# First stage of a three-stage attention kernel: per-tile x loads, mask product last, weight split one slot later, another order of the first loads

## The chip, the cores and the metric

The kernel runs on one core of a Trainium2 chip. The metric is the device time of one execution in microseconds (us); lower is better. Engines are named as the profile names them: PE (TensorE), DVE (VectorE), ACT (ScalarE), POOL (GpSimd) and SP (SyncE, which here only issues DMAs).

## What is computed

The input x holds 32 batches of 64 tokens by 512 features, and each batch has its own 256 context rows of 512 features and a mask. Three blocks follow one another, each added to its input:

```
x = x + cross_attention(layernorm(x), ctx, mask)   # scores over 256 context rows, softmax, read-out
x = x + latent_attention(layernorm(x), weights)    # low-rank q and kv, rotary part, 16 heads, causal
x = x + ffn(layernorm(x), weights)                 # square of relu, an expert sum, a layernorm
```

Everything is float32. Products that must be exact are made as three products of a rounded part and a remainder ("hi" and "lo").

## The kernel before

Three stages run one after another: `phase_x`, `phase_m` and `phase_f`. Only `phase_x` is touched. It does the cross-attention, the second layernorm and the low-rank projection z. Its unit is a pair of batches, that is 128 tokens, so there are 16 pairs. All 16 tiles of x (256 KB each) have a place of their own in `x_all`; the context rows (`ctx_in`, 1 MB a pair) and their transpose (`ctxT`, 1 MB a pair) have two places each, used in turn.

Every engine runs its own list of instructions, slot by slot, and semaphores tie the lists together. `slots` calls slot 0 to 18: slots 0 to 2 and 13 to 18 are written out, and those between run in a loop. The pairs are staggered. In slot p:

- PE: scores of pair p, read-out of p-1, transpose of the normalised x of p+1, projection of p-2, transpose of the probabilities of p, transpose of the second norm of p-1 (`turn1`, which waits for ACT's `norm`). Only then come the scores of p+1.
- DVE: remainder of the probabilities of p-1 (`probs_lo`), remainder of the second transpose (`turned1_lo`), layernorm statistics of x of pair p+2 (`first_var`), `latent_var`, `maximum` of the scores of p, `residual` and second statistics of p-1, then smaller work.
- POOL: half of the remainder of the context of p (`ctx_split`), 1/sqrt of the variance for p+2 (`rstd_of(0, p+2)`, from `first_var`), `latent_rstd`, the other half of `ctx_split`, `rstd_of(1, p-1)` (from the second statistics), `rotate(p-3)`.
- ACT: `probs_hi`, `turned1_hi`, first norm of p+1, squares, `exp`, `scale_q`, copy of the transposed x, `ctx_round` of p+1 (1.9 us), second norm of p-1.
- SP: in this order, load of `ctxT` for p+2 (after the scores of p), store of z of p-3 (after `rotate(p-3)`), store of the x of p-1 (after `residual`), load of `ctx_in` for p+2 (after all of `ctx_split(p)`).

Before slot 0, SP issues the first loads, in the order of the diff's minus and context lines; the last is x of pairs 4 to 15 in one DMA of 3 MB (line 172). The latent weights `w_raw` (1.1 MB) are rounded by ACT and their remainder is made by DVE at the end of slot 0 (lines 339 and 353). The scores begin with a small product that puts in the mask (line 500), which needs the loaded table `picks`.

Of the kernel before, what the change touches and what calls it, by code (L numbers as in the profile page):

```python
# [28 lines left out]
KH = HID // P  # L29
# [32 lines left out]
def phase_x(nc, A, scratch, early):  # L62

    with ExitStack() as ctx:
# [12 lines left out]
        def bank(name):  # L77
# [39 lines left out]
        b_z = [bank("z0"), bank("z1")]  # L117

        s = {n: ctx.enter_context(nc.semaphore("x_" + n)) for n in (
            "x_first x_second x_third x_rest masks_loaded small_loaded w_loaded ctxT_first0 ctxT_first1 ctxT_loaded0 ctxT_loaded1 "  # L120
            "ctx_loaded0 ctx_loaded1 x1_stored "
            "z_stored0 z_stored1 pool_setup consts masks_built w_hi w_lo "
            "stats0 var0 eps0 rstd0 shift0 norm0 turned0 xT0 stats1 var1 eps1 rstd1 shift1 norm1 turned1 xT1_hi xT1_lo "
# [13 lines left out]
        def has(p):  # L137

            return not isinstance(p, int) or 0 <= p < PAIRS
# [10 lines left out]

        @block.sync
        def _(sp):
            sp.dma_start(x_all[:, 0], x_t[0]).then_inc(s["x_first"], 16)
            for h in range(2):
                sp.dma_start(ctxT[:, 0, 2 * h:2 * h + 2], A["ctx_turned"][0, :, 2 * h:2 * h + 2]).then_inc(s[f"ctxT_first{h}"], 16)
            sp.dma_start(mask_u8[:], A["mask_BxS2_bk0"]).then_inc(s["masks_loaded"], 16)
            sp.wait_ge(s["pool_setup"], 2)
            sp.dma_start(picks[0:BATCH + 2].rearrange("p a n -> p (a n)"), A["picks"]).then_inc(s["masks_loaded"], 16)
            sp.dma_start(x_all[:, 1], x_t[1]).then_inc(s["x_second"], 16)
            sp.dma_start(ctx_in[:, 0], A["ctx_rows"][0]).then_inc(s["ctx_loaded0"], 16)  # L160
            sp.dma_start(ctxT[:, 1], A["ctx_turned"][1]).then_inc(s["ctxT_loaded1"], 16)
            sp.dma_start(x_all[:, 2:4], x_t[2:4].rearrange("t p d -> p t d")).then_inc(s["x_third"], 16)
            sp.dma_start(w_raw[:], A["w_latent"].rearrange("(k p) n -> p k n", p=P)).then_inc(s["w_loaded"], 16)
            sp.dma_start(ctx_in[:, 1], A["ctx_rows"][1]).then_inc(s["ctx_loaded1"], 16)
            for half in range(2):
                rows = slice(SEQ * half, SEQ * half + SEQ)
                sp.dma_start(cos[rows, :], A["rope_cos"]).then_inc(s["small_loaded"], 16)
                sp.dma_start(sin[rows, :], A["rope_sin"]).then_inc(s["small_loaded"], 16)
            sp.dma_start(qkv_b[:, 0:QLR], bcast_rows(A["L0_attn_wq_a_b"])).then_inc(s["small_loaded"], 16)
            sp.dma_start(qkv_b[:, QLR:ZW], bcast_rows(A["L0_attn_wkv_a_b"])).then_inc(s["small_loaded"], 16)  # L170
            sp.dma_start(kv_w[:], bcast_rows(A["L0_attn_kv_norm_w"])).then_inc(s["small_loaded"], 16)
            sp.dma_start(x_all[:, 4:], x_t[4:].rearrange("t p d -> p t d")).then_inc(s["x_rest"], 16)

            def load_ctxT(p, par):
                sp.wait_ge(s["scored"], p - 1)
                sp.dma_start(ctxT[:, par], A["ctx_turned"][p]).then_inc(s[f"ctxT_loaded{par}"], 16)

            def load_ctx(p, par):
                sp.wait_ge(s["ctx_lo"], 4 * (p - 1))
                sp.dma_start(ctx_in[:, par], A["ctx_rows"][p]).then_inc(s[f"ctx_loaded{par}"], 16)  # L180

            def store_z(p, par):
                sp.wait_ge(s["z_kv"], p + 1)
                sp.wait_ge(s["z_rope"], p + 1)
                sp.wait_ge(s["q_scaled"], p + 1)
                sp.dma_start(z_t[p], zbuf[:, par]).then_inc(s[f"z_stored{par}"], 16)

            def slot(p, par):
                if isinstance(p, int) and p == PAIRS - 1:
                    early.start(sp)  # L190
                if has(p + 2):
                    load_ctxT(p + 2, par)
                if has(p - 3):
                    store_z(p - 3, 1 - par)
                if has(p - 1):
                    sp.wait_ge(s["x1_done"], p)
                    sp.dma_start(x1_t[p - 1], x_all[:, p - 1]).then_inc(s["x1_stored"], 16)
                if has(p + 2):
                    load_ctx(p + 2, par)

            slots(sp, slot)
            for par in range(2):
                sp.wait_ge(s[f"z_stored{par}"], 8 * PAIRS)
            sp.wait_ge(s["x1_stored"], 16 * PAIRS)
# [66 lines left out]
        def _(act):  # L271
# [47 lines left out]
            def slot(p, par):  # L319
                if has(p - 1):  # L320
                    probs_hi(p - 1)
                if has(p - 2):
                    turned1_hi(p - 2)
                if has(p + 1):
                    norm(0, p + 1, xn0, x_all[:, p + 1])
                if has(p - 3):
                    squares(p - 3, 1 - par)
                if has(p):
                    exp(p)
                if has(p - 3):  # L330
                    scale_q(p - 3, 1 - par)
                if has(p + 1):
                    turned0(p + 1)
                    ctx_round(p + 1, 1 - par)
                if has(p - 1):
                    norm(1, p - 1, xn1, x_all[:, p - 1])
                if isinstance(p, int) and p == 0:
                    act.wait_ge(s["w_loaded"], 16)
                    a.copy(w_hi[:].rearrange(flat), w_raw[:].rearrange(flat)).then_inc(s["w_hi"], 1)

# [6 lines left out]
        def _(dve):  # L347
# [7 lines left out]
            def var(k, p, src):  # L355

                n = count(dve, held, p + 1)
                v.bn_stats(stats[k][:], src).then_inc(s[f"stats{k}"], 1)
                dve.wait_ge(s["x_first"], 16)
                dve.wait_ge(s[f"shift{k}"], p)  # L360
                dve.wait_ge(s[f"stats{k}"], n)
                v.bn_aggr(mean_var[k][:], stats[k][:]).then_inc(s[f"var{k}"], 1)
                dve.wait_ge(s[f"var{k}"], p + 1)
                if k == 0:
                    v.tensor_scalar(var_eps[k][:], mean_var[k][:, 1:2], float(HID), HID * 1e-5, ALU.mult, ALU.add).then_inc(s["eps0"], 1)
                else:
                    v.tensor_scalar(var_eps[k][:], mean_var[k][:, 1:2], 1e-5, None, ALU.add).then_inc(s["eps1"], 1)

            def first_var(p):
                if isinstance(p, int):  # L370
                    dve.wait_ge(s["x_first" if p < 1 else "x_second" if p < 2 else "x_third" if p < 4 else "x_rest"], 16)
                else:
                    dve.wait_ge(s["x_rest"], 16)
                var(0, p, x_all[:, p])

            def latent_var(p):
# [35 lines left out]
            def residual(p):  # L412
                dve.wait_ge(s["read"], p + 1)
                dve.wait_ge(s["validated"], p + 1)
                v.scalar_tensor_tensor(x_all[:, p], b_read[:], rvalid[:], x_all[:, p], ALU.mult, ALU.add).then_inc(s["x1_done"], 1)
                dve.wait_ge(s["x_first"], 16)
                dve.wait_ge(s["x1_done"], p + 1)
                var(1, p, x_all[:, p])

# [10 lines left out]
            def slot(p, par):  # L430
# [2 lines left out]
                if has(p - 2):  # L433
                    turned1_lo(p - 2)
                if has(p + 2):
                    first_var(p + 2)
                if has(p - 3):
                    latent_var(p - 3)
                if has(p):
# [6 lines left out]
                    latent_kv(p - 3, 1 - par)  # L446
                if has(p - 2):
                    bias(p - 2, par)
                if isinstance(p, int) and p == 0:
                    dve.wait_ge(s["w_hi"], 1)  # L450
                    split(w_lo[:].rearrange(flat), w_raw[:].rearrange(flat), w_hi[:].rearrange(flat), s["w_lo"])

            first_var(0)
            dve.wait_ge(s["masks_loaded"], 32)
            v.tensor_scalar(mask_rows[0:BATCH].rearrange("r (h m) -> r h m", h=2),
                            mask_u8[:].unsqueeze(1).broadcast_to([BATCH, 2, CTX]), BIG, -BIG,
                            ALU.mult, ALU.add).then_inc(s["masks_built"], 1)
            first_var(1)
            slots(dve, slot)

        @block.tensor
        def _(pe):
# [30 lines left out]
            def score(p, par):  # L493
                pe.wait_ge(s["xT0"], p + 1)
                pe.wait_ge(s["exped"], p)
                if isinstance(p, int) and p == 0:
                    pe.wait_ge(s["masks_built"], 1)
                else:
                    pe.wait_ge(s[f"ctxT_loaded{par}"], 8 * (p + par))
                t.matmul(b_score[:], picks[:, p].bitcast(BF16), mask_rows, start=True, stop=False)  # L500
                for k in range(KH):
                    if isinstance(p, int) and p == 0 and k % 2 == 0:
                        pe.wait_ge(s[f"ctxT_first{k // 2}"], 16)
                    mm = t.matmul(b_score[:], xnT0[:, k], ctxT[:, par, k], start=False, stop=k == KH - 1)
                mm.then_inc(s["scored"], 1)

            def read(p, par):
# [1190 lines left out]
```

## Time and profile before

| | us |
|---|---|
| median of three runs | 1302.01 (1300.41 to 1304.21) |
| profiled execution, its own time | 1296.42 |
| profiled execution, span | 1294.6 |
| PE busy in the span | 1197.3 (92%) |
| first stage | about 0 to 217 |

In the rows below a timeline row gives start, duration, engine, line, operation, the tiles written and read, and in brackets how long the engine had been idle and what ended it. "SPq" rows are DMA issues: their duration is that of the issue and not of the transfer. "DMA to landing" is the time from issue until the data are there. In a row of stretches each engine has its busy time and its number of instructions; then come the granted clock of TensorE as a share of 2.4 GHz, the mean busy share of the DMA engines, and GB/s.

### The profile page before, as it was taken

The numbers are of one execution on the slowest core, as the hardware profiler recorded it, in microseconds if no ns is written. First come the engines' busy times: TensorE is split into PE (matmuls) and PEld (weight loads), VectorE is DVE, ScalarE is ACT, GpSimd is POOL, SyncE is SP. The second block draws the span as 40 slices with busy tenths as digits, with TensorE's granted clock in tenths as the row PEclk, the third lists the DMA queues.
The fourth block names the chain that finished last, engine by engine and source line by source line (L and its number), as shares of the span: only waits on it lengthen the run. The fifth ranks groups of instructions, "written<-read, shape, count | busy, mean of one in ns | idle before, by whom it ended". The sixth has DMA issues, their size and how long they took to land. (4 is left out here: it accounts for less than half of the span.)

```text
span 1294.6 us, 21520 instructions
## 1 busy us (share of the span) xinstructions
PE 1197.3 (92%) x8001; PEld 1055.2 (82%) x8001; DVE 656.2 (51%) x1249; ACT 448.5 (35%) x847; POOL 433.5 (33%) x473
## 2 busy tenths in 40 slices
PE   4899996779999999999999999848999999999996
PEld 2677775558999999999999999647899899899895
DVE  2455553546555666555656665336535345353342
ACT  3566662533333333333333333225222122131220
POOL 3577673412222222222222221204234243252351
PEclk9999999889999999999999999969999999999998
DMA  9566653630010101010000000082000000000000
GB/s 352 207 246 217 217 201 131 241 103 13 7 48 1 53 0 53 0 50 3 21 32 20 32 1 33 1 278 81 17 17 34 1 33 32 0 32 19 15 18 17
DMA packets 37920, 93.04 MB, mean 72 GB/s; under 512 B 7734, under 2 KB 12233, under 8 KB 33131
## 3 DMA queue, kind: packets, MB, share of 16 engines
q1 hardware_dynamic: 37866, 92.33, 20.4%
q8 instruction: 34, 0.56, 0.2%
q14 instruction: 20, 0.16, 0.0%
HBM read 75.02 MB, written 17.30 MB: 71 GB/s over the span
## 5 line engine op out<-in xcount | busy, mean ns | idle before, releaser
L701 POOL TENSOR_TENSOR m_rot<-m_rot,m_rot_b 128x512 f32<-128x512 f32 x32 | 41.5, 1298 | 410.7 <-DVE m_rot_b L858 410.7
L43 PE MATMUL f_b_u<-f_xnT_lo,f_up_hi 128*128 128x256 f32 x512 | 146.3, 286 | 4.7 <-DVE f_up_lo L1487 4.7
L44 PE MATMUL f_b_u<-f_xnT_hi,f_up_lo 128*128 128x256 f32 x512 | 145.9, 285 | 0.0
L45 PE MATMUL f_b_u<-f_xnT_hi,f_up_hi 128*128 128x256 f32 x512 | 145.9, 285 | 0.0
L1399 POOL TENSOR_TENSOR f_hT_lo<-f_h,f_hT_hi 128x512 fp32r<-128x512 f32 x64 | 86.0, 1344 | 106.2 <-ACT f_hT_hi L1441 106.2
L45 PE MATMUL m_b_q<-m_zT_hi,m_wq_hi 128*128 128x256 f32 x384 | 107.0, 279 | 0.0
L43 PE MATMUL m_b_q<-m_zT_lo,m_wq_hi 128*128 128x256 f32 x384 | 106.8, 278 | 0.0
L44 PE MATMUL m_b_q<-m_zT_hi,m_wq_lo 128*128 128x256 f32 x384 | 106.8, 278 | 0.0
L43 PE MATMUL m_b_w<-m_wvo_lo,m_oT_hi 128*128 128x512 f32 x256 | 103.9, 406 | 2.0 <-DVE m_oT_lo L828 2.0
L43 PEld LDWEIGHTS f_b_u<-f_xnT_lo,f_up_hi 128*128 128x128 f32 x512 | 99.4, 194 | 5.9 <-issue 5.6
L43 PE MATMUL f_b_d<-f_down_lo,f_hT_hi 128*128 128x512 f32 x256 | 101.3, 396 | 1.5 <-POOL f_hT_lo L1399 0.9
L1511 DVE TENSOR_TENSOR f_h<-f_h 128x512 f32<-128x512 f32 x64 | 71.7, 1121 | 58.8 <-ACT f_h L1438 58.8
L45 PE MATMUL m_b_w<-m_wvo_hi,m_oT_hi 128*128 128x512 f32 x256 | 100.8, 394 | 0.0
L44 PE MATMUL m_b_w<-m_wvo_hi,m_oT_lo 128*128 128x512 f32 x256 | 100.2, 391 | 0.0
L45 PE MATMUL f_b_d<-f_down_hi,f_hT_hi 128*128 128x512 f32 x256 | 99.8, 390 | 0.0
L44 PE MATMUL f_b_d<-f_down_hi,f_hT_lo 128*128 128x512 f32 x256 | 99.7, 389 | 0.0
L44 PEld LDWEIGHTS f_b_u<-f_xnT_hi,f_up_lo 128*128 128x128 f32 x512 | 99.4, 194 | 0.3
L45 PEld LDWEIGHTS f_b_u<-f_xnT_hi,f_up_hi 128*128 128x128 f32 x512 | 99.3, 194 | 0.0
L231 POOL TENSOR_TENSOR x_ctx_lo<-x_ctx_in,x_ctx_hi 128x512 fp32r<-128x512 f32 x64 | 80.6, 1280 | 6.5 <-ACT x_ctx_hi L294 6.1
L1441 ACT CAST f_hT_hi<-f_h 128x512 fp32r<-128x512 f32 x64 | 39.7, 621 | 110.3 <-DVE f_h L1511 110.3
L828 DVE TENSOR_TENSOR m_oT_lo<-m_b_q,m_oT_hi 128x512 fp32r<-128x512 f32 x64 | 41.2, 685 | 71.7 <-ACT m_oT_hi L784 70.9
L1039 PE MATMUL m_b_s<-m_keys,m_qT_hi 128*128 128x128 f32 x256 | 72.8, 284 | 1.6 <-issue 1.6
(202 smaller groups left out, 3272.0 us busy)
## 6 DMA issues: line engine op xcount, KB each, us to landing
x_ctx_in<-ctx_rows_dram SPq DMA_DIRECT2D x16, 1024.0 KB, 5.0
x_ctxT<-ctx_turned_dram SPq DMA_DIRECT2D x15, 1024.0 KB, 4.9
z_scratch<-x_zbuf SPq DMA_DIRECT2D x16, 288.0 KB, 2.1
m_z_in<-z_scratch SPq DMA_DIRECT2D x8, 576.0 KB, 3.7
x_scratch<-x_x_all SPq DMA_DIRECT2D x16, 256.0 KB, 2.4
m_x<-x_scratch SPq DMA_DIRECT2D x8, 512.0 KB, 3.6
x_scratch<-m_x SPq DMA_DIRECT2D x8, 512.0 KB, 2.8
f_x<-x_scratch SPq DMA_DIRECT2D x8, 512.0 KB, 3.7
```

Of the source, the lines that this page charges most:

```text
L43: nc.tensor.matmul(out, lh, rl, start=first, stop=False)
L44: nc.tensor.matmul(out, ll, rh, start=False, stop=False)
L45: return nc.tensor.matmul(out, lh, rh, start=False, stop=last)
L231: g.tensor_tensor(ctx_lo[:, par, m], ctx_in[:, par, m], ctx_hi[:, par, m].bitcast(F32), ALU.subtract).then_inc(s["ctx_lo"], 1)
L701: q.tensor_tensor(rot[:], rot[:], rot_b[:], ALU.add).then_inc(s["rot_ready"], 1)
L828: v.tensor_tensor(lo, src, hi.bitcast(F32), ALU.subtract).then_inc(done, 1)
L1039: t_.matmul(out, qT_hi[:, m, 2 * j + b].rearrange("p h q -> p (h q)"), nope, start=n == 0, stop=False)
L1399: g.tensor_tensor(hT_lo[:, 2 * n:2 * n + 2].rearrange("p m n -> p (m n)"), h[:, n % 2], hT_hi[:, 2 * n:2 * n + 2].bitcast(F32).rearrange(" ...
L1441: a.copy(hT_hi[:, 2 * n:2 * n + 2].rearrange("p m n -> p (m n)"), h[:, n % 2]).then_inc(s["h_hi"], 1)
L1511: v.tensor_tensor(h[:, n % 2], h[:, n % 2], h[:, n % 2], ALU.mult).then_inc(s["squared"], 1)
```

## The change

- x is no longer loaded in pieces of 1, 1, 2 and 12 tiles with four semaphores, but a tile at a time with a semaphore for even and one for odd pairs. Tiles 0 to 2 are loaded before slot 0. Tile p+3 is issued by SP at the end of its slot p, behind the context load of p+2 (`load_x`).
- In the first loads the context rows of pair 1 come ahead of the latent weights. The seven small loads (rotary tables, biases, norm weight) move to the end of SP's slot 0 (`load_small`).
- The latent weights are rounded and split in slot 1 and not in slot 0.
- The mask product is the last of the group of nine matmuls that makes the scores, and in pair 0 the wait for the mask is just before it.

```
             sp.dma_start(ctxT[:, 1], A["ctx_turned"][1]).then_inc(s["ctxT_loaded1"], 16)
-            sp.dma_start(x_all[:, 2:4], x_t[2:4].rearrange("t p d -> p t d")).then_inc(s["x_third"], 16)
+            sp.wait_ge(s["x_loaded0"], 16)
+            sp.dma_start(x_all[:, 2], x_t[2]).then_inc(s["x_loaded0"], 16)
+            sp.dma_start(ctx_in[:, 1], A["ctx_rows"][1]).then_inc(s["ctx_loaded1"], 16)
             sp.dma_start(w_raw[:], A["w_latent"].rearrange("(k p) n -> p k n", p=P)).then_inc(s["w_loaded"], 16)
-            sp.dma_start(ctx_in[:, 1], A["ctx_rows"][1]).then_inc(s["ctx_loaded1"], 16)
-            (seven small loads)
-            sp.dma_start(x_all[:, 4:], x_t[4:].rearrange("t p d -> p t d")).then_inc(s["x_rest"], 16)
+            def load_small():
+                (seven small loads)
+            def load_x(p, par):
+                sp.wait_ge(s[f"x_loaded{par}"], 8 * (p - par))
+                sp.dma_start(x_all[:, p], x_t[p]).then_inc(s[f"x_loaded{par}"], 16)
...
                 if has(p + 2):
                     load_ctx(p + 2, par)
+                if has(p + 3):
+                    load_x(p + 3, 1 - par)
+                if isinstance(p, int) and p == 0:
+                    load_small()
...
-                if isinstance(p, int) and p == 0:
+                if isinstance(p, int) and p == 1:
                     act.wait_ge(s["w_loaded"], 16)
                     a.copy(w_hi[:].rearrange(flat), w_raw[:].rearrange(flat)).then_inc(s["w_hi"], 1)
...
-            def first_var(p):
+            def first_var(p, par):
+                dve.wait_ge(s[f"x_loaded{par}"], 8 * (p - par) + 16)
                 var(0, p, x_all[:, p])
...
-                if isinstance(p, int) and p == 0:
+                if isinstance(p, int) and p == 1:
                     dve.wait_ge(s["w_hi"], 1)
                     split(w_lo[:].rearrange(flat), w_raw[:].rearrange(flat), w_hi[:].rearrange(flat), s["w_lo"])
...
-                if isinstance(p, int) and p == 0:
-                    pe.wait_ge(s["masks_built"], 1)
-                else:
+                if not (isinstance(p, int) and p == 0):
                     pe.wait_ge(s[f"ctxT_loaded{par}"], 8 * (p + par))
-                t.matmul(b_score[:], picks[:, p].bitcast(BF16), mask_rows, start=True, stop=False)
                 for k in range(KH):
...
-                    mm = t.matmul(b_score[:], xnT0[:, k], ctxT[:, par, k], start=False, stop=k == KH - 1)
+                    t.matmul(b_score[:], xnT0[:, k], ctxT[:, par, k], start=k == 0, stop=False)
+                if isinstance(p, int) and p == 0:
+                    pe.wait_ge(s["masks_built"], 1)
+                mm = t.matmul(b_score[:], picks[:, p].bitcast(BF16), mask_rows, start=False, stop=True)
                 mm.then_inc(s["scored"], 1)
```

## Rows read from the trace of the kernel before

**Rows 1.** Busy time by stretch: start-up, and the first and last full stretch of steady slots.

```profile
20.00:40.00 20.00, 9.66 (x33) 6.13 (x33) 8.01 (x14) 9.46 (x11) 9.40 (x12) 0.83 0.98 366
60.00:80.00 20.00, 19.07 (x104) 14.52 (x103) 11.71 (x31) 13.26 (x24) 14.33 (x23) 1.00 0.60 215
...
180.00:200.00 20.00, 19.88 (x98) 14.46 (x97) 8.92 (x21) 11.46 (x23) 14.31 (x21) 1.00 0.53 194
```

**Rows 2.** Timeline of the start-up, all engines: loads and what waited for them.

```profile
15.93 0.65 SPq L172 DMA_DIRECT2D x_x_all<-x_dram  x1
...
18.16 0.69 DVE L358 BATCH_NORM_STATS2 x_stats<-x_x_all 128x6 f32<-128x512 f32 x1 [5.13 <-DMA x_x_all<-x_dram]
...
24.00 1.90 ACT L294 CAST x_ctx_hi<-x_ctx_in 128x2048 fp32r<-128x2048 f32 x1 [2.74 <-DMA x_ctx_in<-ctx_rows_dram]
...
25.81 2.11 ACT L339 CAST x_w_hi<-x_w_raw 128x2304 fp32r<-128x2304 f32 x1
...
27.95 2.94 DVE L353 TENSOR_TENSOR x_w_lo<-x_w_raw,x_w_hi 128x2304 fp32r<-128x2304 f32 x1 [6.19 <-ACT x_w_hi L339]
...
38.26 1.90 ACT L294 CAST x_ctx_hi<-x_ctx_in 128x2048 fp32r<-128x2048 f32 x1 [1.17 <-DMA x_ctx_in<-ctx_rows_dram]
...
46.37 0.80 PE L43 MATMUL x_read<-x_ctx_lo,x_pT_hi 128*128 128x512 f32 x1
...
54.34 0.39 PE L500 MATMUL x_score<-x_picks 128*128 128x512 bf16 x1
```

**Rows 3.** Timeline of SP: the first and last of eleven z stores, and one slot's issues.

```profile
65.61 0.37 SPq L186 DMA_DIRECT2D z_scratch<-x_zbuf  x1
...
135.41 0.36 SPq L186 DMA_DIRECT2D z_scratch<-x_zbuf  x1
136.06 0.36 SPq L197 DMA_DIRECT2D x_scratch<-x_x_all  x1
136.60 0.35 SPq L180 DMA_DIRECT2D x_ctx_in<-ctx_rows_dram  x1
...
181.38 0.35 SPq L186 DMA_DIRECT2D z_scratch<-x_zbuf  x1
```

**Rows 4.** Timeline of DVE around the end of a steady slot.

```profile
130.88 0.75 DVE L415 SCALAR_TENSOR_TENSOR x_x_all<-x_read,x_rvalid,x_x_all 128x512 f32 x1 [2.19 <-PE x_read L45]
...
132.88 0.15 DVE L367 TENSOR_SCALAR x_var_eps<-x_mean_var 128x1 f32<-128x1 f32 x1
...
137.17 0.68 DVE L358 BATCH_NORM_STATS2 x_stats<-x_x_all 128x6 f32 x1
...
139.43 0.69 DVE L401 TENSOR_REDUCE x_negmax<-x_score 128x1 f32<-128x512 f32 x1 [0.93 <-PE x_score L504]
```

**Rows 5.** Timeline of POOL around the same place.

```profile
133.12 0.54 POOL L222 TENSOR_TENSOR x_rstd<-x_var_eps,x_neg_half 128x1 f32<-128x1 f32 x1 [2.13 <-DVE x_var_eps L367]
...
134.87 0.32 POOL L250 TENSOR_TENSOR x_zbuf<-x_rope_tmp 128x64 f32<-128x64 f32 x1
...
138.44 0.54 POOL L222 TENSOR_TENSOR x_rstd<-x_var_eps,x_neg_half 128x1 f32<-128x1 f32 x1 [0.78 <-DVE x_var_eps L365]
...
140.06 2.54 POOL L231 TENSOR_TENSOR x_ctx_lo<-x_ctx_in,x_ctx_hi 128x512 fp32r<-128x512 f32 x2
```

**Rows 6.** Timeline of PE at the same slot's end.

```profile
134.22 0.60 PE L468 MATMUL x_prob<-x_ident,x_probs 128*128 128x128 f32 x4
135.09 0.66 PE L468 MATMUL x_turn<-x_ident,x_xn 128*128 128x128 f32 x4 [0.27 <-ACT x_xn L278]
```

**Rows 7.** Landing of the context loads of line 180, window 60 to 200.

```profile
DMA to landing us min/median/max: 4.8/4.9/5.2
```

**Rows 8.** Landing of the x loads and x stores, window 0 to 60.

```profile
DMA to landing us min/median/max: 2.6/6.7/17.4
```

**Rows 9.** Busy time and clock of two other stretches.

```profile
42.00:44.00 2.00, 2.00 (x3) 0.75 (x3) 1.66 (x5) 0.92 (x2) 0.74 (x1) 0.50 0.07 29
...
280.00:300.00 20.00, 15.51 (x135) 14.33 (x134) 11.17 (x25) 8.72 (x19) 6.09 (x5) 1.00 0.18 60
```

More of the change, by code:

```diff
@@ L119, in phase_x @@
         s = {n: ctx.enter_context(nc.semaphore("x_" + n)) for n in (
-            "x_first x_second x_third x_rest masks_loaded small_loaded w_loaded ctxT_first0 ctxT_first1 ctxT_loaded0 ctxT_loaded1 "
+            "x_loaded0 x_loaded1 masks_loaded small_loaded w_loaded ctxT_first0 ctxT_first1 ctxT_loaded0 ctxT_loaded1 "
             "ctx_loaded0 ctx_loaded1 x1_stored "
@@ L152, in _ @@
         def _(sp):
-            sp.dma_start(x_all[:, 0], x_t[0]).then_inc(s["x_first"], 16)
+            sp.dma_start(x_all[:, 0], x_t[0]).then_inc(s["x_loaded0"], 16)
             for h in range(2):
@@ L158, in _ @@
             sp.dma_start(picks[0:BATCH + 2].rearrange("p a n -> p (a n)"), A["picks"]).then_inc(s["masks_loaded"], 16)
-            sp.dma_start(x_all[:, 1], x_t[1]).then_inc(s["x_second"], 16)
+            sp.dma_start(x_all[:, 1], x_t[1]).then_inc(s["x_loaded1"], 16)
             sp.dma_start(ctx_in[:, 0], A["ctx_rows"][0]).then_inc(s["ctx_loaded0"], 16)
             sp.dma_start(ctxT[:, 1], A["ctx_turned"][1]).then_inc(s["ctxT_loaded1"], 16)
-            sp.dma_start(x_all[:, 2:4], x_t[2:4].rearrange("t p d -> p t d")).then_inc(s["x_third"], 16)
+            sp.wait_ge(s["x_loaded0"], 16)
@@ L163, in _ @@
+            sp.dma_start(x_all[:, 2], x_t[2]).then_inc(s["x_loaded0"], 16)
+            sp.dma_start(ctx_in[:, 1], A["ctx_rows"][1]).then_inc(s["ctx_loaded1"], 16)
             sp.dma_start(w_raw[:], A["w_latent"].rearrange("(k p) n -> p k n", p=P)).then_inc(s["w_loaded"], 16)
-            sp.dma_start(ctx_in[:, 1], A["ctx_rows"][1]).then_inc(s["ctx_loaded1"], 16)
[L165 to L168, printed above, removed]
@@ L169, in _ @@
-            sp.dma_start(qkv_b[:, 0:QLR], bcast_rows(A["L0_attn_wq_a_b"])).then_inc(s["small_loaded"], 16)
-            sp.dma_start(qkv_b[:, QLR:ZW], bcast_rows(A["L0_attn_wkv_a_b"])).then_inc(s["small_loaded"], 16)
-            sp.dma_start(kv_w[:], bcast_rows(A["L0_attn_kv_norm_w"])).then_inc(s["small_loaded"], 16)
-            sp.dma_start(x_all[:, 4:], x_t[4:].rearrange("t p d -> p t d")).then_inc(s["x_rest"], 16)
+            def load_small():
+                for half in range(2):
+                    rows = slice(SEQ * half, SEQ * half + SEQ)
+                    sp.dma_start(cos[rows, :], A["rope_cos"]).then_inc(s["small_loaded"], 16)
+                    sp.dma_start(sin[rows, :], A["rope_sin"]).then_inc(s["small_loaded"], 16)
+                sp.dma_start(qkv_b[:, 0:QLR], bcast_rows(A["L0_attn_wq_a_b"])).then_inc(s["small_loaded"], 16)
+                sp.dma_start(qkv_b[:, QLR:ZW], bcast_rows(A["L0_attn_wkv_a_b"])).then_inc(s["small_loaded"], 16)
+                sp.dma_start(kv_w[:], bcast_rows(A["L0_attn_kv_norm_w"])).then_inc(s["small_loaded"], 16)
@@ L358, in var @@
                 v.bn_stats(stats[k][:], src).then_inc(s[f"stats{k}"], 1)
-                dve.wait_ge(s["x_first"], 16)
+                dve.wait_ge(s["x_loaded0"], 16)
                 dve.wait_ge(s[f"shift{k}"], p)
@@ L367, in var @@
                     v.tensor_scalar(var_eps[k][:], mean_var[k][:, 1:2], 1e-5, None, ALU.add).then_inc(s["eps1"], 1)
-            def first_var(p):
-                if isinstance(p, int):
-                    dve.wait_ge(s["x_first" if p < 1 else "x_second" if p < 2 else "x_third" if p < 4 else "x_rest"], 16)
-                else:
-                    dve.wait_ge(s["x_rest"], 16)
+            def first_var(p, par):
+                dve.wait_ge(s[f"x_loaded{par}"], 8 * (p - par) + 16)
                 var(0, p, x_all[:, p])
@@ L415, in residual @@
                 v.scalar_tensor_tensor(x_all[:, p], b_read[:], rvalid[:], x_all[:, p], ALU.mult, ALU.add).then_inc(s["x1_done"], 1)
-                dve.wait_ge(s["x_first"], 16)
+                dve.wait_ge(s["x_loaded0"], 16)
                 dve.wait_ge(s["x1_done"], p + 1)
@@ L435, in slot @@
                 if has(p + 2):
-                    first_var(p + 2)
+                    first_var(p + 2, par)
                 if has(p - 3):
@@ L448, in slot @@
                     bias(p - 2, par)
-                if isinstance(p, int) and p == 0:
+                if isinstance(p, int) and p == 1:
                     dve.wait_ge(s["w_hi"], 1)
                     split(w_lo[:].rearrange(flat), w_raw[:].rearrange(flat), w_hi[:].rearrange(flat), s["w_lo"])
-            first_var(0)
+            first_var(0, 0)
             dve.wait_ge(s["masks_loaded"], 32)
@@ L457, in _ @@
                             ALU.mult, ALU.add).then_inc(s["masks_built"], 1)
-            first_var(1)
+            first_var(1, 1)
             slots(dve, slot)
@@ L495, in score @@
                 pe.wait_ge(s["exped"], p)
-                if isinstance(p, int) and p == 0:
-                    pe.wait_ge(s["masks_built"], 1)
-                else:
+                if not (isinstance(p, int) and p == 0):
                     pe.wait_ge(s[f"ctxT_loaded{par}"], 8 * (p + par))
-                t.matmul(b_score[:], picks[:, p].bitcast(BF16), mask_rows, start=True, stop=False)
                 for k in range(KH):
```

## The prediction, made before the changed kernel was run

> **What bounds the kernel now.** The changed code lies in the first 217 us, so I read the busy time by stretch first, then the timeline of each engine in the start-up and in one steady slot, and last the landing times of the loads. Two regimes show. In the start-up (0 to 40 us) the DMA engines are 98% busy at 366 GB/s and PE works half the time; from 60 to 200 us PE is 95 to 99% busy and the DMA engines 53 to 60% [rows 1]. So bytes set the pace until about 40 us, and PE after it. The steady slot's length is the distance of z stores: ten slots from 65.61 to 181.38, 11.58 us each [rows 3].
>
> PE's cover in the steady slot is thin. Its last step waits for the second norm, here 0.27 us, and the next scores are queued behind that step [rows 6]. That norm comes from POOL's rstd at 133.12, which waits for DVE's statistics [rows 4, 5]. Whatever delays that rstd stalls PE by nearly as much. This is where I look for the cost.
>
> **The x tiles in the steady slots.** I count from R, the end of POOL's rotation, 134.87 + 0.32 = 135.19 [rows 5]. SP is released by it and issues the z store at 135.41, the x store at 136.06 and the context load at 136.60, that is R+1.41 [rows 3]. The new x load is the next on the same queue: one spacing (0.54) later, R+1.95. It carries pair p+3, and DVE's statistics of that pair stand early in the very next slot: they ran at 137.17, R+1.98 [rows 4]. Before, those data had long been there. Now the load is issued in the same moment in which it is wanted.
>
> When does it land? The context load ahead of it takes 4.9 us (4.8 to 5.2) [rows 7], so it lands at R+6.3. Behind it, 0.262 MB at the 366 GB/s of a full queue is 0.7 us [rows 1]: R+7.0, and with 0.1 for the release R+7.1. That the queue serves in order is what the start-up shows: the context rows of pair 2 sat behind the 3 MB of x and were first used at 38.26 [rows 2].
>
> From the landing the cycle closes on itself:
> - statistics to POOL's rstd: 138.44 - 137.17 = 1.27, giving R+8.4;
> - rstd to the second half of the context split: 140.06 - 138.44 = 1.62 [rows 5], R+10.0;
> - the split: 2.54, R+12.5;
> - the rstd of the second norm to the next rotation's end: 135.19 - 133.12 = 2.07 [rows 5], next R at R+14.6.
>
> DVE could be later than the split. After its statistics (1.3) and about 0.3 of small work come the maximum (0.69) and, the read-out being done by then, residual and second statistics (130.88 to 133.03, 2.15) [rows 4]: R+7.1+1.3+0.3+0.7+2.15 = R+11.6, before R+12.5. So POOL's queue closes the loop. With some spacing between steps I take 14.7 us for a slot in place of 11.58: 3.1 us each. PE's 11.3 us of work (11.58 less the 0.27 of waiting) fit in 14.7, with about 3 us idle before each second-norm transpose.
>
> How often: tiles 3 to 15 come this way. Those of slots 0 to 2 are issued before any z store and are counted below. Tiles 6 to 15, issued in slots 3 to 12, lengthen ten slots: 10 x 3.1 = 31 us. Nothing later gives this back, since PE has no reserve of work and the next stage starts when this one has ended.
>
> Bounds of a slot: the first x load of the kernel, on an empty queue, landed in 2.6 us [rows 8]. With that, R+1.95+2.6 = R+4.55, plus 1.27+1.62+2.54+2.07 is 12.05, a loss of 0.5 a slot, 5 us. Above: R+7.1 plus the same cycle with a context landing at 5.2 and 0.3 more of queueing, 15.2, 36 us.
>
> **The start-up.** The 3.15 MB load (15.93) leaves the place ahead of pair 2's context [rows 2]; at 366 GB/s it takes 8.6 us. In turn each x tile becomes a wait of its own. Step by step:
> - x of pair 2 now loads without pair 3: 0.7 us earlier than 18.16, so maximum and exp of slot 0 are 0.7 earlier. DVE's wait for this tile stands ahead of the maximum, so the scores of pair 0, though they no longer wait for the mask table and end some 2.5 us earlier, bring nothing more. The nine matmuls are the same in number and size; the other order is costed at nothing, and from slot 1 on the mask has long been there.
> - context rows of pair 1 ahead of 1.18 MB of weights and without 0.26 MB of x: 3.9 us earlier than 24.00, some 20.1; ACT can take them at 20.5.
> - weights out of slot 0: ACT's 2.11 and DVE's 2.94 no longer stand ahead of the first probabilities [rows 2], so these are ready at 23.7 (20.5, the rounding 1.90, two copies of about 0.65) instead of 31.6 (27.95 + 2.94 + 0.7).
> - but x of pair 3 is issued only after the context split of pair 0 (about 22.4), behind transposed context 2 and context rows 2. By bytes it lands at about 29.7. DVE's slot 1 waits for it, with maximum and residual behind. Rstd at 31.0 (1.27), split from 32.0 to 34.5, rstd, shift and second norm to 36.3, transpose 0.66, scores of pair 2 at 37.0, where before they came at about 41.6 (38.26 + 1.90, then norm and transpose, 1.5).
> - then the weights: ACT from 36.3, DVE until 41.4. Only then can DVE give the remainder of pair 1's probabilities (42.1), and the read-out starts at about 42.5 instead of 46.37 [rows 2].
> - x of pair 4 (about 40) and pair 5 (about 53.2, issued at 48.1) land at or within 1 us of when they are wanted.
>
> The read-out being 3.9 us ahead, the scores of pair 3 start near 50.6 instead of 54.34 [rows 2]: a gain of 3.7. Bounds: 0, if the small loads and late x tiles eat it, and 8.6, the whole of the removed transfer. I take the chain's 3.7, since the waits in it are named. The small loads, now behind x of pair 3, are first wanted by the bias add of slot 2, over 15 us after issue; costed at nothing under that cover, at most the 1.2 us that their 0.43 MB take at 366 GB/s.
>
> **Sum.** -3.7 + 31 = +27.3. Against the profiled execution: 1296.4 + 27.3 = 1323.7. The median of the three runs lies 5.6 above that execution; so 1302.0 + 27.3 = 1329.
>
> **Rivals.**
> (A) The above, x behind the context rows in one queue: 1329. For it: the order of issue, the queue in the start-up, and the POOL cycle.
> (B) The x tile overtakes the 1 MB load and lands as on an empty queue: 10 x 0.5 - 3.7 = +1.3, 1303. For it only the 2.6 us row; against it the start-up. The Trainium skill speaks for B's possibility ("DMA: Bandwidth & Descriptors", Two DMAs through the same engine are not ordered): it warns that DMAs on one queue start in order but that nothing orders them across the 16 engines. Where this would let the small tile through, the time would be B's.
> (C) The other side, faster: the x wait is under cover and the start-up gives all 8.6 us, 1293.4. The point that decides: the tile must land early enough for the split to end before the second rstd, whose place is 133.12+11.58-135.19 = R+9.5. So landing by R+9.5-2.54-1.62-1.27 = R+4.1, which is 2.1 us after its issue. No x load here was that quick [rows 8]; it would need an earlier issue than the SP order allows.
> (D) PE's idle time costs clock as well. After 4 us of idleness the stretch at 42 to 44 us has a granted clock of 0.50, the 1.2 GHz level [rows 9]. If scores and read-out ran at that level throughout, they would take about 12.3 us from R+0.4, residual and statistics after it 2.2, then 2.1 of POOL: 17.1 a slot, 10 x 5.5 - 3.7 = +51, 1353. Against it: at 280 to 300 us PE is 78% busy, as it would be here (11.3 of 14.7), with a granted clock of 1.00 [rows 9]. A low clock for only the first 3 us or so would stay under POOL's cycle.
>
> **Chances and range.** A 0.78, B 0.08, C 0.05, D 0.09. Within A the slot's bounds of 14.3 to 15.2 and the start-up's 0 to 8.6 give +18 to +36, 1320 to 1338. The range leaves out B and C and takes in part of the way to B (a landing between) and to D (some clock lost): 1313 to 1345. A change under 0.3% (3.9 us) can't be told from none in this kernel; so slower 0.87, same 0.08, faster 0.05.
>
> **What the profile after should show.** DVE's statistics of line 358 idle about 5 us in each slot from pair 6 on, with DMA x as releaser; the z stores about 14.7 us apart for ten slots, then 11.6 or less again; POOL's second-norm rstd no longer waiting for DVE's statistics but queued behind the split; PE idle some 3 us before the second-norm transpose; scores of pair 3 near 50.6. Wrong if the x tile lands at R+4.5 or earlier (B), if the granted clock in the loop is near 0.5 in most of a slot (D), or if another queue member, such as the transposed context behind the x tile, becomes late instead.

## The result and the profile after

The changed kernel takes 1331.4 us (median of four runs, 1327.4 to 1333.0). Its ratio to the kernel before is 1.022, with a 95% interval of 1.0186 to 1.0254: slower by 29.4 us against the 1302.0 of the kernel before; whether by more than 2%, the interval leaves open. One run of the kernel before in this comparison was disturbed (2996 us) and is left out of the ratio and of that median.

The busy time of the loop, which answers to [rows 1]. The columns are the stretch, its length, busy time and instructions of PE, PE's weight loads, DVE, ACT and POOL, then the granted clock, the DMA share and GB/s:

```profile
60.00:80.00 20.00, 14.22 (x67) 9.90 (x67) 9.75 (x22) 11.17 (x21) 12.77 (x22) 0.95 0.49 177
180.00:200.00 20.00, 17.14 (x67) 11.45 (x69) 8.93 (x21) 10.81 (x22) 12.18 (x21) 0.83 0.54 180
```

PE was 95 to 99% busy in these two stretches and is now 71 and 86% busy. The DMA engines moved less per second than before (177 and 180 GB/s against 215 and 194), so over a whole slot it isn't bandwidth that ran out. SP's timeline, answering to [rows 3], gives the first and last of the eleven z stores of the loop, and one slot's issues:

```profile
62.57 0.37 SPq L192 DMA_DIRECT2D z_scratch<-x_zbuf  x1
...
137.53 0.35 SPq L192 DMA_DIRECT2D z_scratch<-x_zbuf  x1
138.09 0.35 SPq L203 DMA_DIRECT2D x_scratch<-x_x_all  x1
138.62 0.35 SPq L186 DMA_DIRECT2D x_ctx_in<-ctx_rows_dram  x1
139.21 0.35 SPq L178 DMA_DIRECT2D x_x_all<-x_dram  x1
...
212.02 0.35 SPq L192 DMA_DIRECT2D z_scratch<-x_zbuf  x1
```

Ten slots in 149.45 us: 14.95 each instead of 11.58. The new load stands last. The slot that follows, on DVE (the statistics of x, then the maximum, the residual's statistics) and on POOL:

```profile
144.69 0.69 DVE L368 BATCH_NORM_STATS2 x_stats<-x_x_all 128x6 f32 x1 [5.28 <-DMA x_x_all<-x_dram]
...
146.04 0.69 DVE L408 TENSOR_REDUCE x_negmax<-x_score 128x1 f32<-128x512 f32 x1
...
148.63 0.15 DVE L377 TENSOR_SCALAR x_var_eps<-x_mean_var 128x1 f32<-128x1 f32 x1
```

```profile
145.96 0.55 POOL L232 TENSOR_TENSOR x_rstd<-x_var_eps,x_neg_half 128x1 f32<-128x1 f32 x1 [6.05 <-DVE x_var_eps L375]
...
147.67 2.52 POOL L241 TENSOR_TENSOR x_ctx_lo<-x_ctx_in,x_ctx_hi 128x512 fp32r<-128x512 f32 x2
150.15 0.58 POOL L232 TENSOR_TENSOR x_rstd<-x_var_eps,x_neg_half 128x1 f32<-128x1 f32 x1
...
151.95 0.32 POOL L260 TENSOR_TENSOR x_zbuf<-x_rope_tmp 128x64 f32<-128x64 f32 x1
```

DVE stood idle 5.28 us until the tile landed, and POOL 6.05 us behind it. The rstd of the second norm (150.15) has no bracket: it waited for nothing but the split in front of it in POOL's own queue. Its input had been ready since 148.78. At the slot's end PE waits for the norm that comes from there:

```profile
152.17 0.66 PE L475 MATMUL x_turn<-x_ident,x_xn 128*128 128x128 f32 x4 [3.52 <-ACT x_xn L288]
152.66 5.30 PE L508 MATMUL x_score<-x_ctxT,x_xnT 128*128 128x512 f32 x8
```

The waits of the loop in total, the same story in the view of waits (60 to 220 us; total, times, longest):

```profile
POOL x_rstd L232 <- DVE x_var_eps L375: 61.9, 10, 6.5
DVE x_stats L368 <- DMA x_x_all<-x_dram: 53.0, 10, 5.6
...
PE x_turn L475 <- ACT x_xn L288: 29.2, 11, 3.8
```

Where the 36.6 us between the two profiled spans (1294.6 and 1331.2) lie follows from landmarks of both traces. Until the first z store the changed kernel is 3.0 ahead (62.57 against 65.61); the ten slots cost 33.7 (149.45 against 115.77); from the eleventh z store to the last one of this stage, 1.4 more (36.53 from 212.02 to 248.55, against 35.11), all of it in the first slot of these (12.61 against 11.19); the end of the stage, to the first matmul of the next one, 2.7 (10.89 against 8.19); and 1.8 come in the two stages behind. That 1.8 can't be put down to the change: the code of these two stages is the same in all fourteen kernels of this document, and from their first matmul to the end they took between 1069.9 (the kernel before) and 1076.6 us (1071.8 in the changed kernel). The medians differ by 29.4 and not by 36.6, since the profiled execution of the kernel before was 5.6 under its median and that of the changed kernel 1.6 above.

### The profile page after: what moved, and what is told of

It is laid out like the page before. It is cut to its first block and busy times, and to the rows that moved or that the text cites. A ratio compares the mean times of both kernels' runs of the same rounds, so it can differ in the third digit from the quotient of the medians.

```text
span 1331.2 us, 21548 instructions
## 1 busy us (share of the span) xinstructions
PE 1214.6 (91%) x7987; PEld 1064.5 (80%) x8001; DVE 666.4 (50%) x1249; ACT 448.0 (34%) x847; POOL 433.5 (33%) x473
## 5 line engine op out<-in xcount | busy, mean ns | idle before, releaser
L708 POOL TENSOR_TENSOR m_rot<-m_rot,m_rot_b 128x512 f32<-128x512 f32 x32 | 41.5, 1298 | 412.2 <-DVE m_rot_b L865 412.2
```

Source lines behind the costliest of these rows:

```text
L708: q.tensor_tensor(rot[:], rot[:], rot_b[:], ALU.add).then_inc(s["rot_ready"], 1)
```

## The experiments

R is the end of POOL's rotation as in the prediction. For each kernel the start of the first z store tells how long the start-up took, and a tenth of the distance from there to the eleventh is the slot; both are read from one profiled execution. Each ratio is to the runs of the kernel before in the same group, whose medians differ by 1.1 us, so small differences between versions are compared by the ratios.

| kernel | us, median | ratio (95%) | first z store | slot |
|---|---|---|---|---|
| before | 1301.3 to 1302.5 by group | | 65.61 | 11.58 |
| changed | 1331.4 | 1.022 (1.0186 to 1.0254) | 62.57 | 14.95 |
| x load first in SP's slot | 1293.8 | 0.9944 (0.9928 to 0.9959) | 58.79 | 11.54 |
| x load ahead of context load | 1297.6 | 0.997 (0.9958 to 0.9982) | 58.70 | 11.92 |
| x in one piece | 1308.2 | 1.005 (1.0031 to 1.0068) | 73.18 | 11.55 |
| split first on POOL | 1316.8 | 1.0116 (1.0095 to 1.0138) | 59.85 | 13.82 |
| x behind 2 MB | 1364.5 | 1.0481 (1.0457 to 1.0505) | 67.65 | 17.79 |
| statistics late | 1291.1 | 0.9921 (0.9899 to 0.9944) | 56.31 | 11.59 |
| x first, mask product first | 1293.3 | 0.9928 (0.991 to 0.9946) | 56.67 | 11.56 |
| x first, weights in slot 0 | 1296.2 | 0.9953 (0.9936 to 0.9969) | 59.46 | 11.56 |
| late x tiles alone | 1334.4 | 1.0264 (1.0242 to 1.0286) | 65.76 | 14.87 |
| mask product last alone | 1300.9 | 1.000 (0.9989 to 1.001) | 67.28 | 11.55 |
| both orders | 1292.0 | 0.9935 (0.992 to 0.995) | 57.81 | 11.57 |
| statistics late, mask first | 1291.4 | 0.9931 (0.9915 to 0.9947) | 56.55 | 11.56 |

### The x load a slot earlier

```
                     early.start(sp)
+                if has(p + 3):
+                    load_x(p + 3, 1 - par)
                 if has(p + 2):
                     load_ctxT(p + 2, par)
...
                     load_ctx(p + 2, par)
-                if has(p + 3):
-                    load_x(p + 3, 1 - par)
```

> Edit: the x load of pair p+3 is the first thing in SP's slot p and no longer the last, a whole slot earlier. Theory Q (a late x tile closes a cycle through SP and POOL): the ten slots return from 14.95 to 11.6 us, DVE's statistics have no wait for x in the loop, and with the start-up's gain of 3 us or more the time is 1294 to 1300. Rival O (the other parts of the change cost the time: mask product last, weights in slot 1, first loads): slots stay over 14 us, 1325 to 1332. Rival T (256 KB more traffic a slot slows the context loads): slots of 12 to 13 us, 1305 to 1315.

Measured: 1293.8, slots of 11.54, below the expected range by 0.2. The loads are as many and as large as in the changed kernel; only their place differs. So neither the extra traffic per slot (rival T) nor the other parts (rival O) cost the time. SP's slot begins where the slot before it ends, so the x load still stands right behind a context load:

```profile
117.76 0.35 SPq L186 DMA_DIRECT2D x_ctx_in<-ctx_rows_dram  x1
118.68 0.35 SPq L178 DMA_DIRECT2D x_x_all<-x_dram  x1
```

It also takes about as long to land, 5.0 us (4.7 to 5.3) in the loop. What has changed is which tile it carries: one that is wanted a slot later. So this run moves the time of issue alone and not what stands ahead in the DMA queue. DVE's statistics in the loop carry no wait:

```profile
118.46 0.68 DVE L368 BATCH_NORM_STATS2 x_stats<-x_x_all 128x6 f32 x1
```

### The x load just ahead of the context load

```
+                if has(p + 3):
+                    load_x(p + 3, 1 - par)
                 if has(p + 2):
                     load_ctx(p + 2, par)
-                if has(p + 3):
-                    load_x(p + 3, 1 - par)
```

> Edit: in SP's slot the x load of p+3 goes just ahead of the context load of p+2 instead of just behind it; both are issued at the slot's end. Theory Q: with no 1 MB ahead the tile lands behind the x store alone, at about R+1.4+2.6 = R+4.0 to R+4.5 instead of R+7.3; the slot is 12.0 to 12.5 us by the same POOL cycle, or 11.6 where PE binds; total loss over the loop 0 to 9 us, time 1300 to 1310. If landing did not depend on what is ahead in the queue (rival B of the prediction), the slot would shorten by only the 0.6 us of earlier issue, to 14.3: about 1325.

Measured: 1297.6, below the expected 1300 to 1310, with slots of 11.92 where 12.0 to 12.5 were expected. The landing of the x loads in the loop, first in the changed kernel, then here:

```profile
DMA to landing us min/median/max: 4.9/5.2/5.5
```

```profile
DMA to landing us min/median/max: 2.6/2.7/2.8
```

The load is issued only 0.6 us earlier in the slot, but lands 2.5 us sooner after its issue. That difference is the 1 MB in front of it. The tile is still late here: DVE waits 2.24 us for it, and a wait that long costs only 0.3 to 0.4 us a slot. With R at 118.16, DVE starts on the tile at R+4.3 (122.48). The prediction's rival B had priced just that: R+4.55 and a slot of 12.05. So the price of B was about right; what rules it out for the changed kernel is that the tile did not overtake the context load there.

```profile
119.52 0.35 SPq L178 DMA_DIRECT2D x_x_all<-x_dram  x1
120.05 0.35 SPq L186 DMA_DIRECT2D x_ctx_in<-ctx_rows_dram  x1
```

```profile
122.48 0.69 DVE L368 BATCH_NORM_STATS2 x_stats<-x_x_all 128x6 f32 x1 [2.24 <-DMA x_x_all<-x_dram]
```

### 2 MB ahead of the tile

```
                 if has(p + 3):
+                    sp.wait_ge(s["again"], 16 * p)
+                    sp.dma_start(again[:], A["ctx_rows"][p + 2]).then_inc(s["again"], 16)
                     load_x(p + 3, 1 - par)
```

> Edit: the changed kernel with the context rows of p+2 loaded a second time, into a tile that nothing reads, between the context load and the x load: 2 MB ahead of the tile instead of 1 MB. Theory Q (landing time behind what is queued, passed on one to one by the cycle): the tile lands 1.05 MB / 366 GB/s = 2.9 us later, slots of 14.95+2.9 = 17.8 us, ten of them: about 1331+29 = 1360 (1354 to 1366). If the wait were set by something other than the bytes ahead, slots stay near 15 us and the time near 1331 to 1336.

Measured: 1364.5, slots of 17.79, that is 2.84 longer for 1.05 MB more; the tile lands 7.4 us after its issue (6.8 to 8.1). The three doses, 0, 1 and 2 MB ahead of the tile, give slots of 11.92, 14.95 and 17.79. The first step, 3.03, holds the 0.6 us of earlier issue too; so each MB ahead costs 2.4 to 2.8 us a slot, once the slack is used up.

### x in one piece

```
+                    sp.wait_ge(s["x_loaded0"], 32)
+                    sp.dma_start(x_all[:, 3:], x_t[3:].rearrange("t p d -> p t d")).then_inc(s["x_loaded0"], 16)
```

This stands behind the small loads in slot 0, in place of the loads per slot.

> Edit: x of pairs 3 to 15 in one DMA behind the small loads in slot 0, the rest of the change kept. Theory Q: slots of 11.6 us again. The 3.3 MB stand ahead of the transposed context of pair 3 only; start-up gain 0 to 4 us: 1298 to 1303. Rival O: 1325 or more.

The loop is back at 11.55, as theory Q has it. The time, 1308.2, lies over the expected 1298 to 1303: x of pair 3 is in that piece, and DVE's slot 1 waits for all of it.

```profile
41.30 0.69 DVE L368 BATCH_NORM_STATS2 x_stats<-x_x_all 128x6 f32<-128x512 f32 x1 [17.26 <-DMA x_x_all<-x_dram]
```

So one piece removes the cost in the loop, but it must not hold a tile that is wanted soon: the first z store comes at 73.18, against 62.57 in the changed kernel and 65.61 in the kernel before, whose last piece began with pair 4.

### The context split ahead of the rstd that waits

```
                 if has(p):
                     ctx_split(p, par, (2, 3))
                 if has(p + 2):
                     rstd_of(0, p + 2)
                 if has(p - 3):
                     latent_rstd(p - 3)
                 if has(p - 1):
                     rstd_of(1, p - 1)
```

> Edit: on POOL the second half of the context split comes before the rstd of pair p+2 (the one that waits for the x tile); loads as in the changed kernel. Theory Q: the split (2.5 us) leaves the chain behind the tile; the cycle is then tile landed R+7.4, DVE's second statistics R+11.5, POOL 2.1: R+13.7, that is 1.3 us less a slot than 14.95, time about 1318 (1315 to 1322). If the wait for the tile were not passed on through POOL's order, nothing would change: 1331.

Measured: 1316.8, slots of 13.82 against 13.7 reckoned. The tile lands as late as before, but the split's 2.5 us no longer stand behind it. POOL in one such slot:

```profile
115.85 4.97 POOL L241 TENSOR_TENSOR x_ctx_lo<-x_ctx_in,x_ctx_hi 128x512 fp32r<-128x512 f32 x4
124.58 0.54 POOL L232 TENSOR_TENSOR x_rstd<-x_var_eps,x_neg_half 128x1 f32<-128x1 f32 x1 [3.76 <-DVE x_var_eps L375]
...
127.48 0.54 POOL L232 TENSOR_TENSOR x_rstd<-x_var_eps,x_neg_half 128x1 f32<-128x1 f32 x1 [1.26 <-DVE x_var_eps L377]
```

The second norm's rstd waits for DVE again, as expected: DVE's queue, not POOL's, now carries the delay on.

### Statistics late on DVE and POOL

```
 DVE:   latent_var(p - 3), maximum(p), residual(p - 1), first_var(p + 2, par), validate(p), ...
 POOL:  ctx_split(p; 0, 1), latent_rstd(p - 3), ctx_split(p; 2, 3), rstd_of(1, p - 1), rotate(p - 3), rstd_of(0, p + 2)
```

`maximum` also waits for `validated` of the pair before, which its old place had made sure of.

> Edit: x loads exactly as in the changed kernel, late; but DVE makes the statistics of p+2 after maximum and residual, and POOL their rstd last in its slot, behind both split halves, the second norm's rstd and the rotation. Theory Q: the tile lands at R+7.4 as before, but nothing that the next slot's end needs stands behind it; slots of 11.5 to 11.9 us, time 1294 to 1303. If a late tile cost time whatever the order (by DMA traffic or memory), slots stay near 15 us: 1325 or more.

Measured: 1291.1, under the expected 1294 to 1303; slots of 11.59. SP issues the tile in the same place as the changed kernel, as late as there:

```profile
104.10 0.35 SPq L186 DMA_DIRECT2D x_ctx_in<-ctx_rows_dram  x1
104.76 0.35 SPq L178 DMA_DIRECT2D x_x_all<-x_dram  x1
```

```profile
109.78 0.75 DVE L423 SCALAR_TENSOR_TENSOR x_x_all<-x_read,x_rvalid,x_x_all 128x512 f32 x1 [2.19 <-PE x_read L45]
...
112.13 0.69 DVE L368 BATCH_NORM_STATS2 x_stats<-x_x_all 128x6 f32 x1 [0.20 <-issue]
```

DVE takes the tile at 112.13, 7.4 us after its issue, and waits for no data. So a tile that is issued late costs nothing by itself; what stands behind the wait in the engines' queues costs. The first z store is at 56.31, since in the start-up too the maximum of a pair no longer stands behind the next tile.

### Late tiles alone, on the kernel before

```
-            sp.dma_start(x_all[:, 4:], x_t[4:].rearrange("t p d -> p t d")).then_inc(s["x_rest"], 16)
...
                     load_ctx(p + 2, par)
+                if has(p + 3):
+                    load_x(p + 3, 1 - par)
```

Tiles 0 to 2 are loaded ahead of slot 0; the order of the other first loads, the weights and the mask product are as before.

> Edit: the kernel before with only the x loads changed: tiles 0 to 2 ahead of slot 0, x of p+3 last in SP's slot; mask product first, weights in slot 0, small loads and first order as before. Theory Q: the ten slots are 14.9 to 15.0 us by this edit alone, +33 to +34; the start-up gains only some 1 us since the context rows of pair 1 still come behind the weights: 1334 to 1340, slower than the full change. Rival O (the other parts carry the loss): under 1310.

Measured: 1334.4, slots of 14.87. This one part carries the whole loss, 33 us, and the start-up gains nothing by it (65.76 against 65.61). So what makes the change's start-up 3 us shorter is the rest of the change: the mask product, the weights and the order of the other first loads. No run tests that order alone.

### The other parts, one at a time

Mask product put back as first, in the version with the x load first:

> Edit: the version with the x load first in SP's slot, and the mask product put back as the first of its group with its wait. The wait for the mask table (11.7) delays the scores of pair 0 from 8.8, but the maximum behind them waits for x of pair 2 (18.0) anyway: 0 to 0.5 us, 1294. If the mask product's place has a price of its own (matmul order in the group), it shows in 16 slots: 0.2 us each would be 3 us.

Weights put back into slot 0, in the same version:

```
-                if isinstance(p, int) and p == 1:
+                if isinstance(p, int) and p == 0:
                     act.wait_ge(s["w_loaded"], 16)
...
-                if isinstance(p, int) and p == 1:
+                if isinstance(p, int) and p == 0:
                     dve.wait_ge(s["w_hi"], 1)
```

> Edit: the version with the x load first in SP's slot, and the weight rounding and split back in slot 0. DVE's 2.6 to 2.9 us then stand ahead of the first probabilities (23.2 becomes about 28) but no longer ahead of those of pair 1: 0 to 3 us slower, 1294 to 1297. If the later slot had cost time, it would be faster than 1293.8.

Mask product last alone, on the kernel before:

```
-                t.matmul(b_score[:], picks[:, p].bitcast(BF16), mask_rows, start=True, stop=False)
                 for k in range(KH):
...
+                mm = t.matmul(b_score[:], picks[:, p].bitcast(BF16), mask_rows, start=False, stop=True)
```

> Edit: the kernel before with only the mask product moved to the end of its group. The scores of pair 0 end earlier but DVE still waits for x of pair 2 before the maximum, and PE idles longer before pair 1's scores, which in the other kernels with the mask last ran 1.1 to 1.8 us longer. Here the slot-0 weight split on DVE (until 31) hides that: no change, 1300 to 1304. If the place of the product had a price in each slot, 3 us or more would show.

Mask product put back as first, in the version with late statistics:

> Edit: statistics late, and the mask product put back as the first of its group. With the statistics late, the maximum of pair 0 no longer waits for x of pair 2, so here the mask table (landed 11.7 to 12.4) does hold back the scores of pair 0, by about 3.5 us; against it the shorter idle time of PE before pair 1's scores gives back 1 to 2 us. Expected within 2 us of 1291, on either side.

Measured, in this order: 1293.3, 1296.2, 1300.9 and 1291.4. The first is 0.7 under the 1294 expected, the others lie in their ranges. The place of the mask product can't be told from no change (1.000 alone; 0.9928 beside 0.9944; 0.9931 beside 0.9921). With the weights in slot 0 the ratio is 0.9953 beside 0.9944 and the first z store 0.7 us later (59.46 against 58.79); the intervals overlap, so a cost of the earlier slot is not shown.

### Both repairs together

> Edit: statistics late on DVE and POOL, and the x load first in SP's slot. Theory Q: each of the two removes the whole stall, so the two together bring nothing over one: slots of 11.6 us, 1289 to 1293. If slack were still short with the late tile, it would be faster than 1290.

Measured: 1292.0, slots of 11.57. The two don't add. The fastest version is the one with late statistics, 1291.1, or 0.8% below the kernel before; the others near it are within its interval. In all of them the loop is where PE binds, and only the start-up differs.

## Why the prediction was right

The forecast was 1329 (1313 to 1345) with slower at 0.87; measured was 1331.4. Point by point:

- **The place of the load.** Foretold issue R+1.95 and landing R+7.1. With R at 137.32 the issue is at 139.21 (R+1.9) and DVE starts on the tile at 144.69 (R+7.4). That it lands behind the 1 MB is shown by the doses, and by the landing times in the loop: never under 4.9 us. Rival B, that the tile overtakes, would have needed R+4.55; the tile lands so only when nothing large is ahead.
- **The cycle through POOL.** Foretold 14.7, measured 14.95, 31 against 33.7 us for ten slots. The sum round the cycle was R+14.6, taken as 14.7 for some spacing; in the slot shown DVE starts on the tile 0.3 later than R+7.1 (R+7.4), and the steps from there to the next R take 7.6 us and not 7.5. That POOL's split closes the loop and DVE's statistics come 1.4 us sooner (0.9 foretold) is in the rows (148.78 against 150.15), and split first took off 1.1 of the 1.3 us reckoned.
- **Ten slots, and nothing given back.** So it was: slot 3 to slot 13.
- **The start-up.** Foretold gain 3.7, measured 3.0 at the first z store, and that agreement is in part two misses that offset each other. The chain was right to within 1.2 us at its main points: x of pair 3 was taken at 29.02 (29.7 foretold), the scores of pair 2 began at 36.60 (37.0), the weights were done at 40.23 (41.4), the scores of pair 3 began at 49.72 (50.6), 4.6 ahead and not 3.7. But x of pair 5, said to be late by 1 us at most, was late by 3:

```profile
54.44 0.69 DVE L368 BATCH_NORM_STATS2 x_stats<-x_x_all 128x6 f32 x1 [3.02 <-DMA x_x_all<-x_dram]
```

```profile
52.00:54.00 2.00, 2.00 (x7) 1.08 (x7) 0.00 (x0) 0.24 (x2) 0.00 (x0) 1.00 0.08 29
```

  It was issued 1.3 us earlier than reckoned (46.76) and landed 1.0 later (foretold 53.2), since it took 7.4 us and not 5.1. The context load just ahead of it took 7.2 us, where 5.2 is the median in the loop, and the transposed context of pair 4, issued at 42.36, landed only at 48.1; so more stood ahead of the tile than the prediction counted. That doesn't explain all of it: from 52 to 54 us the DMA engines were 8% busy together and the tile was still not there. Why is open. By this wait the first z store is 3.0 ahead of the kernel before, where the scores of pair 3 had been 4.6 ahead (49.72 against 54.34).
- **What was costed at nothing.** The mask product's place: right in the runs' medians, but the traces show a cost by the clock in the start-up (last section). The small loads behind x of pair 3: right, no bias add waits for them.
- **The clock (rival D).** It fell, but not as priced. In the slot shown above, after 3.52 us of idleness, PE's scores took 5.30 us where the kernel before had 3.60 in each slot looked at, and the stretch at their start has a granted clock of 0.52. The slot didn't grow by it, since POOL's cycle is longer, as the prediction had argued. Outside the loop, where PE binds, the loss shows: 1.4 us in the slot after the eleventh z store, and the 2.7 at the stage's end (last section). The 1.4 is in these two rows, which in a slot at the full clock are 0.66 and 3.60:

```profile
211.67 1.12 PE L475 MATMUL x_turn<-x_ident,x_xn 128*128 128x128 f32 x4 [3.79 <-ACT x_xn L288]
212.58 4.57 PE L508 MATMUL x_score<-x_ctxT,x_xnT 128*128 128x512 f32 x8
```

  So the prediction's sum had left out a term: rival D priced the clock only in the ten slots. The stretch in the slot shown above:

```profile
153.00:156.00 3.00, 3.00 (x5) 1.34 (x4) 1.00 (x2) 2.14 (x6) 1.73 (x2) 0.52 0.91 284
```

- **The sum.** -3.0 + 33.7 is 30.7 where 27.3 was foretold; the clock's terms and 1.8 us in the later stages bring the profiled pair to 36.6. The medians differ by only 29.4, since the two profiled executions lay 5.6 under and 1.6 above theirs. So the total fits the median within 2.4 us partly by luck: against the profiled pair, the sum was 9.3 short, 2.7 of it in the slots, 0.7 in the start-up, 4.1 in the clock's terms and 1.8 in the later stages, which lie within what these stages vary by from one profiled execution to another (6.7 us in the fourteen). The lower bound of a slot in the prediction's range, 14.3, isn't worked out anywhere in it.

## What to carry to other kernels

A load that is split up must be issued early enough for its first reader, counting what stands ahead of it in the same DMA queue; here 256 KB behind 1 MB needed 5.2 us and without it 2.7, and a full slot of lead took the whole wait away. A wait costs what stands behind it in the queue of the waiting engine and of the engines after it: the same late tile cost 3.4 us a slot, 2.2 with one step moved ahead of it, and nothing with the statistics put last. To price such a wait, follow it until it comes back to the instruction that issued the load; if it does, and the sum round that cycle is more than the slot was, that sum is the new slot.

## What was not expected of the hardware

**Earlier work was followed by slower work.** With the mask product last, the scores of pair 0 are done early and PE then has little to do until the scores of pair 1. Stretches of the version with the x load first, mask product last:

```profile
14.00:17.00 3.00, 0.01 (x1) 0.00 (x0) 0.00 (x0) 2.16 (x2) 0.70 (x3) 1.00 1.01 406
17.00:20.00 3.00, 0.66 (x4) 0.42 (x4) 1.65 (x4) 0.56 (x2) 2.86 (x3) 0.73 1.08 413
...
22.00:24.00 2.00, 2.00 (x3) 0.66 (x2) 0.54 (x1) 2.00 (x3) 1.83 (x2) 0.50 0.27 75
```

The same stretches with the mask product first, where PE waited for the mask table and was at work from 12.7 to 19.7 us:

```profile
14.00:17.00 3.00, 3.00 (x5) 1.30 (x4) 0.00 (x0) 1.92 (x2) 0.79 (x2) 1.00 0.99 404
17.00:20.00 3.00, 2.67 (x8) 1.02 (x6) 1.59 (x4) 0.70 (x1) 2.88 (x3) 1.00 1.02 383
...
22.00:24.00 2.00, 2.00 (x6) 0.95 (x5) 0.33 (x1) 2.00 (x3) 1.84 (x2) 1.00 0.78 323
```

In the first the scores of pair 1 took 5.38 us, at a granted clock of 0.50 (1.2 GHz) until 24 us; in the second they took 3.60 at 1.00 (2.4 GHz). In both they began at 21.64, so the early start of pair 0 had won nothing by then, and the first z store came at 58.79 and 56.67. The other two pairs of versions with the mask product last and first show it as well. On the kernel before, the scores of pair 1 took 5.92 us against 3.60 and the first z store came at 67.28 against 65.61, although its slot-0 weight split had been expected to hide this. With the statistics late they took 5.24 us against 3.60; there they began 2.0 us earlier, but the read-out behind them only 0.14 us earlier (24.15 against 24.29). The time that was won by starting early was lost again through the clock. In the medians of the runs none of these pairs can be told apart.

**A low clock stayed through 6 us of full work.** At the end of the stage, in the changed kernel:

```profile
246.00:249.00 3.00, 3.00 (x13) 3.00 (x14) 0.62 (x3) 0.68 (x2) 1.79 (x5) 0.50 0.18 64
249.00:252.00 3.00, 3.00 (x13) 2.67 (x12) 0.46 (x1) 0.00 (x0) 0.00 (x0) 0.50 0.26 98
```

The clock did not fall while PE was at work. PE had been idle 0.95 us before 243.83 and 1.40 us before 245.89, and the granted clock fell at about 245.25, within the second of these; it stayed at 0.50 until PE stopped at 252. The kernel before had idle times of 0.94 and 1.40 in the same places and ran on at 1.00:

```profile
214.00:217.00 3.00, 3.00 (x23) 3.00 (x24) 1.07 (x4) 0.62 (x1) 1.79 (x5) 1.00 0.16 56
```

With the slower projection of the last pair, the next stage's first matmul came 10.9 us after the last of the z issues (248.55) instead of 8.2 (216.49). Four of the other kernels have part of this loss, 9.5 to 9.7 us (x load first, x ahead, x behind 2 MB, weights in slot 0); the rest show 8.2. What decides it stays open: no experiment here turned it on or off by itself, and the kernel with the late x tiles alone, with slots of 14.87, shows 8.2.
